# Two GpSimd waits on indirect transfers taken out of a fused attention and mixture-of-experts kernel

## What is computed

```
x = x + attention(layernorm(x))          # 16 heads, 3-wide q and k, 8-wide v, causal, softmax
x = x + moe(layernorm(x))                # shared expert + 8 routed experts, top 2 per token

shared = gelu(xf @ Wfc_s + bfc_s) @ Wproj_s + bproj_s        # 128 -> 512 -> 128
probs  = softmax(xf @ Wr);  top 2 of 8, their weights rescaled to sum 1
routed = sum over e of (gelu(xf @ Wfc[e] + bfc[e]) @ Wproj[e] + bproj[e]) * gate[:, e]
moe    = shared + routed
```

## Time and profile before

| | |
|---|---|
| median of 3 runs | 709.67 us (707.07, 709.67, 712.68) |
| the profiled execution's own time | 714.72 us |
| its span in the profile | 713.0 us |
| mean granted TensorE clock | 0.941 of full speed |
| TensorE matmul busy | 592.3 us (83%) |
| VectorE busy | 411.3 us (58%) |
| ScalarE busy | 402.4 us (56%) |
| GpSimd busy | 328.7 us (46%) |

### The profile page before, as it was taken

The page is one execution under the profiler, slowest core; times in us unless marked ns, Lnnn a source line. Parts: engine busy times, 40 slices in busy tenths (PEclk is TensorE's granted clock), DMA queues, the critical chain, the costliest instruction groups (busy, mean ns, idle before and its releaser), DMA issues.

```text
span 713.0 us, 15616 instructions
## 1 busy us (share of the span) xinstructions
PE 592.3 (83%) x5166; PEld 442.1 (62%) x5166; DVE 411.3 (58%) x1135; ACT 402.4 (56%) x723; POOL 328.7 (46%) x441
## 2 busy tenths in 40 slices
PE   2798599989999899998799969999978888857730
PEld 2565366546566566565478957888755676857620
DVE  7799378596788887987744434347643244322222
ACT  4255475556666666685465967795556735414210
POOL 6817142885673783764440141013237554242344
PEclk9799899999999999999999999999998999989875
DMA  5187878101001000102517693767752466768732
GB/s 164 31 258 204 236 244 271 58 16 39 22 4 27 27 10 16 30 20 73 185 31 229 210 278 123 242 218 247 244 183 68 127 216 213 245 184 275 240 98 59
DMA packets 64734, 100.99 MB, mean 142 GB/s; under 512 B 9276, under 2 KB 50016, under 8 KB 64224
## 3 DMA queue, kind: packets, MB, share of 16 engines
q1 hardware_dynamic: 60560, 91.60, 41.8%
q0 software_dynamic: 4096, 8.40, 3.8%
HBM read 83.89 MB, written 32.79 MB: 164 GB/s over the span
## 4 chain that ended last, share of the span: by engine, by line
PE 50%; DVE 18%; issue 13%; DMA 9%; ACT 5%; POOL 3%; another core or an unknown queue 1%; SPq 1%; POOLq 0%; DVEq 0%; ACTq 0%
DVE negmax L1007 10%; PE banks L1313 10%; PE banks L1392 7%; PE banks L1400 7%; PE banks L1295 6%; PE banks L1234 5%; PE banks L1283 5%; DMA xs<-x2n,row 5%; PE banks L1375 3%; PE banks L1370 3%; PE banks L1285 2%; ACT probs L873 2%; DMA got<-ys,from_row 2%; ACT hblk L911 1%; PE banks L1253 1%
## 5 line engine op out<-in xcount | busy, mean ns | idle before, releaser
L1007 DVE TENSOR_REDUCE negmax<-banks 128x2 f32<-128x768 f32 (+3 forms) x192 | 193.0, 1038 | 59.9 <-PE banks L1285 59.3
L873 ACT ACTIVATE probs<-banks 128x1024 f32<-128x1024 f32 (+2 forms) x192 | 157.4, 892 | 44.6 <-PE banks L1295 43.1
L911 ACT ACTIVATE hblk<-banks,wcur 128x128 f32<-128x128 f32 x340 | 95.6, 375 | 97.2 <-PE banks L1392 83.3
L770 POOL DMA_INDIRECT xs<-x2n,row x64 | 63.0, 985 | 157.0 <-DVE row L1091 73.3
L743 POOL TENSOR_SCALAR_AFFINE_SELECT probs<-probs 128x512 f32<-128x512 f32 x128 | 79.8, 640 | 117.5 <-ACT probs L873 116.1
L1283 PE MATMUL banks<-kpad,qst 128*128 128x256 bf16 (+3 forms) x512 | 118.3, 306 | 14.8 <-issue 8.8
L1392 PE MATMUL banks<-xblkT,wcur 128*128 128x128 f32 x680 | 98.0, 291 | 17.2 <-DVE yblk L1148 6.6
L1392 PEld LDWEIGHTS banks<-xblkT,wcur 128*128 128x128 f32 x680 | 88.9, 204 | 25.6 <-issue 11.1
L1400 PE MATMUL banks<-wcur,hblk 128*128 128x128 f32 x680 | 96.0, 288 | 5.9 <-ACT hblk L911 5.1
L1295 PE MATMUL banks<-qmst,kpad 128*128 128x512 bf16 (+3 forms) x512 | 93.3, 305 | 5.6 <-DVE negmax L1007 2.2
L1285 PE MATMUL banks<-future,identb 128*128 128x128 bf16 x512 | 97.0, 222 | 0.0
(11 more groups left out here) (142 smaller groups left out, 777.2 us busy)
## 6 DMA issues: line engine op xcount, KB each, us to landing
wcur<-wtab SPq DMA_DIRECT2D x85, 578.0 KB
xs<-in_L_attn_x SPq DMA_DIRECT2D x8, 1188.0 KB, 7.3
xblk<-xs SPq DMA_DIRECT2D x85, 64.0 KB
ys<-yblk SPq DMA_DIRECT2D x41, 128.0 KB
kpad<-kst SPq DMA_DIRECT2D x64, 64.0 KB, 2.3
xs<-in_L_attn_x SPq DMA_DIRECT2D x8, 505.0 KB
acc<-in_L_attn_x SPq DMA_DIRECT2D x8, 256.0 KB, 5.1
wtab<-in_L_ffn_Wfc SPq DMA_DIRECT2D x2, 1024.0 KB
```

Of the source, the lines that this page charges most:

```text
L770: pool.indirect_dma_start(out=xs[g % 2], out_offset=bass.IndirectOffsetOnAxis(ap=row[:, b % 2, k, i:i + 1], axis=0), in_=x2n[:, b % NX2, i ...
L873: nc.scalar.activation(probs[:, g % 2, heads[0]:heads[-1] + 1, PCOL[tiles]:PCOL[tiles] + P * tiles], unit_view(PLACE["E", b, n], tiles), A ...
L911: ins = nc.scalar.activation(hblk[:, k % 3, q, :], one(PLACE["HB", g, s])[:, P * q:P * q + P], ACT.Gelu_apprx_tanh, bias=wcur[:, k % NW, 2 ...
L1007: dve.tensor_reduce(negmax[:, g, tiles - 1, heads[0]:heads[-1] + 1], unit_view(PLACE["M", b, n], tiles), AX.X, ALU.max, negate=True).then_ ...
```

## The change

In both functions a wait is removed, and nothing else. `send_rows` no longer waits, for tiles 1 to 3 of a batch, until all scatters of this batch issued so far have landed. `get_rows` no longer waits, for tiles 1 to 3 of batches 0 to 6, until the two gathers of the preceding tile have landed (batch 7 never had this wait). All other waits, all lists of steps and all instructions stay. The rows of every engine's program, apart from line numbers and these waits, are the same in the same order.

```
@@ send_rows(b, i)
                 if g >= 2:
                     last = pairs_in(g - 2) - 1
                     pool.wait_ge(xblk_turned, nth("XT", g - 2, last))
-
-                if i > 0:
-                    pool.wait_ge(rows_sent[b % NX2], 16 * (2 * NT * (b // NX2) + 2 * i))
                 for k in range(2):
                     pool.indirect_dma_start(
@@ get_rows(b, i)
                 half_of, j = i // (NT // 2), i % (NT // 2)
                 wait_earlier(pool, out_ready, nth("CB", b - 1, half_of))
-
-                if i > 0 and b < B - 1:
-                    pool.wait_ge(got_rows[(i - 1) // (NT // 2)], 16 * (NT * b + 2 * ((i - 1) % (NT // 2) + 1)))
                 for k in range(2):
                     pool.indirect_dma_start(
```

## The result

The changed kernel takes **663.99 us** (median of 4 runs, 663.6 to 666.7), the kernel before beside it 710.56 us (4 runs). The ratio is 0.9357, with a 95% interval of 0.931 to 0.9404: 46 us less, where 30 us were forecast.

The account below looks back on a forecast made before the run. The prediction took TensorE as the pace in the middle, stalled elsewhere through GpSimd's waits for landings. Terms of 34.7 us, less 5 us given back, left 30 us off 714.7; adjusted to the median, 680 us, 8-in-10 range 667 to 703.

Parts of the forecast that it names:

- The waits were latency, and GpSimd's engine work small: GpSimd's waits are latencies that overlap; a scatter occupies GpSimd for 0.985 us, at a pitch of about 1.28 us.
- Term 1: Batches 4 and 5: PV steps on TensorE held by masks queued behind waiting scatters on GpSimd; 10 us.
- Terms 2 and 3: First block of groups 1 and 2, held by the scatters' landing: 7.4 us and 6 us.
- The rule on completions: Possibility: scatters in flight land after earlier weight loads; first-block gains 2 to 3 us smaller each, forecast 685.
- Term 4: TensorE stalls at 564.22 and 665.85, behind VectorE steps that wait for gathers; 6 us with low clock.
- Term 5: End of the kernel: batch 7's first gather is issued sooner after TensorE is done; 5.3 us.
- Given back: Weights might hold the stretch from 600 to 684, and unseen stalls may appear; 5 us taken off the sum.
- Half given back: Rival: early masks and end hold, other gains mostly go into weights or the next wait; 695 us; chance 0.22.
- same place: Rival: GpSimd's queue works off scatters one at a time, 3.6 us each; 705 to 711 us; chance 0.11.
- slower: Rival: bursts delay block loads of groups 1 and 2, 42 us against 34.7 gained; about 719 us; chance 0.06.
- more than the forecast: Whole kernel: stalls that were not counted go too, below 668 us; chance 0.03.

Follow-up runs that it names:

- the probe: Changed kernel plus, after the last scatter of batches 6 and 7, a GpSimd wait for all eight landings and a clear of one column: 663.36 us, one run.
- e5: Kernel before with all waits kept, four masks moved ahead of a scatter step in GpSimd's list: 698.99 us, ratio 0.9868.
- e13: Kernel before with the waits between scatters out for batches 0 to 3 alone: 709.68 us, ratio 1.002.
- e2: Kernel before with only the waits between gathers out, those between scatters kept: 691.61 us, ratio 0.9729.
- e11: Changed kernel loading only the first 512 of 1156 columns of a block's weights for groups 1 and 2: 658.53 us, ratio 0.9283 to the kernel before.

## Why the prediction was too small

**The waits were latency, and GpSimd's engine work small.** Right. GpSimd's busy time is the same (328.7 and 328.3 us), the pitch of free scatters 1.28 us as taken, and the probe shows that latencies overlap.

**Term 1, masks, 10 us.** Right: 11.8 us (8.4 to 15.2) alone, and the masks were the main mechanism, as e5 shows. That early batches are free was right too (e13).

**Terms 2 and 3, first block of groups 1 and 2, 13.4 us.** Right: 12.2 us (9.2 to 15.2) alone. XB.1.0 went out at 509.5, right behind the weights that SyncE had issued from 507.0 to 508.6, and TensorE waited 0.49 us at XT.1.0, for a copy of VectorE's and not for the block, where I left 1 us. The 2 us of low clock after XT.1.0 also fit: e2, which still has the stall (6.35 us), and the changed kernel, which has not, differ by 2.3 us in the stretch behind it.

**The rule on completions.** I gave as a possibility that scatters in flight land only after the weight loads around them. The Trainium skill, "DMA: Bandwidth & Descriptors", section on queues, rings and completion order, says that the completion increment lands after every earlier write of the same DMA engine. The 5.4 and 5.6 us of the probe are no longer than for a lone pair with weight loads around it, so the burst was stretched no further than a pair is, and the 2 to 3 us that the prediction would have taken off each term were not there. Whether weights in flight are why it is 5.4 us and not the 2.23 us of a quiet queue is not told apart.

**Term 4, gathers that hold VectorE, 6 us.** This is the first step that failed. The mechanism was right, its size was half. I gave it two stalls, 2.22 us at 564 and 2.90 us at 665.9. The stretch up to SC.7 has three stalls with this cause in the kernels that keep the waits, and the low clock that follows them; the landmarks say 11.5 us there (of which 2.3 belong to the low clock after XT.1.0), and 3.7 in the blocks of group 2, together about 13. The runs agree: alone, the gathers of batches 0 to 2 bring 8.9 us (5.1 to 12.8), where my share for them was 3, and all gathers 19.2 us, of which the end has 7.3, so 12 are left for this term. I passed over the third stall because the profile named VectorE's row numbers for it; the wait behind was one step further back, on VectorE's list. The second I could not have read off as a stall of this kind: in the trace that I had, CB.2.0 waited only 0.87 us, and TensorE's 2.86 us at 580 came from ScalarE; in the six other kernels that keep the waits CB.2.0 waited 2.0 to 5.7 us. As far as seven traces tell, that was an accident of one execution, and it hid one of the three stalls.

**Term 5, the end, 5.3 us.** A little small: 7.0 by the landmarks, 7.3 (3.3 to 11.4) alone. The first gather of batch 7 follows TensorE's last block after 2.65 us, not 4.3.

**Given back, 5 us.** The second step that failed, as far as the sum goes. By the landmarks the first block of group 2 and its blocks bring 5.3 + 3.7 = 9.0 us, what term 3 and half of term 4 had before anything was taken off, and the two kinds of wait alone, 24.8 and 19.2 us, already come to 44 of the 46. The DMA share, 0.79, was no ceiling: the kernel before had 0.87 and 277 GB/s for 18 us of the same stretch, and the changed kernel has 0.84 and 268 over 40 us. Yet what I feared is partly there. In the blocks of group 2 TensorE's idle time ahead of first-matrix steps for which the profile names no engine went from 2.4 us (two, at 650 and 660) to 6.4 (the three at 602, 616 and 632), and e11, with fewer bytes of weights, nearly clears these three and gives 3 to 5 us. So weights do take something there; it is made up for by what the gathers' stalls were worth beyond my term 4.

From the 46 us: 30 were forecast; the gathers (terms 4 and 5) brought 19.2 instead of 11.3, which is 8, the part given back is 5, and the rest, 3 us, is within what the runs differ by (1.4 of it in the scatters, 24.8 against 23.4).

**The rivals.** "Half given back", "same place" and "slower" are all excluded by the time; in the mechanism the second is excluded by the probe, the third by XT steps with at most 1.48 us of wait for a block. The chance that I gave to more than the forecast, 0.03, was too small: I had taken 5 us off for gains that are lost and added nothing for stalls that one trace does not name.

## What to carry to other kernels

A wait for a transfer's landing on an in-order engine holds everything behind it for the transfer's latency, and costs time where something behind it is waited for in turn (here not in batches 0 to 3). So read what is queued behind the wait, on that engine and then on each engine that waits for it, down to the one that is the pace. Sum all stalls of a stretch by the cause at the end of the chain, whatever engine the profile names first, and measure a stretch between two landmarks, in more than one trace where there are several: here one execution hid a stall that six other kernels show. A stall also takes with it the low clock behind it. Before taking a back-payment off a sum because a share looks high, look whether the same trace goes higher elsewhere.

## What the runs showed of the hardware

Eight indirect scatters of 128 rows of 512 bytes in flight, at a pitch of 1.28 us and with weight loads around them, land as fast as two: the eighth at most 5.4 and 5.6 us after its issue (one run), the second of a pair 5.79. GpSimd's issue takes 0.985 us on the mean whether transfers are outstanding or not (985 ns in both kernels). The DMA engines held 268 GB/s over 40 us beside the block work, where 245 had looked busy; the kernel before had held 277 GB/s over 18 us.
